# Shared experts as stationary weights over blocks of 512 tokens, and three residual norms worked out tile by tile

## What is computed

```python
x = layernorm(x + attention(x))      # 16 heads of 16, causal; keys and values from a latent of 64; rotary on 12 of 16
t = x                                # (2048, 256)
scores = softmax(t @ gate_w.T)       # 16 experts, the best 2 per token
y = sum over e of swiglu(t, w1[e], w3[e], w2[e]) * weight_e   # inner width 176
z = swiglu(t, sw1, sw3, sw2)         # the shared experts, inner width 352
out = layernorm(x + y + z)
# swiglu(t, a, b, o) = (silu(t @ a.T) * (t @ b.T)) @ o.T
```

## Time and profile before

| what | value |
|---|---|
| time, 3 runs | 842.92 us median (840.75 to 847.7) |
| profiled execution | 841.11 us, of which the span from first to last instruction is 839.4 us |
| mean granted TensorE clock | 0.927 of full speed |
| busy share of the span | PE 87%, PEld 59%, DVE 67%, ACT 48%, POOL 29% |
| DMA | 76.99 MB, mean 92 GB/s |

### The profile page before, as it was taken

How to read it: one execution, slowest core, us unless ns; L and a number is a source line. 1 busy time by engine, 2 the same in 40 slices (tenths; PEclk the granted TensorE clock), 3 DMA queues, 4 the chain that set the end, 5 groups by cost and what they waited for, 6 DMA issues and landing times. The chain is left out here.

```text
span 839.4 us, 14305 instructions
## 1 busy us (share of the span) xinstructions
PE 729.1 (87%) x4309; PEld 491.7 (59%) x4310; DVE 561.3 (67%) x1374; ACT 403.3 (48%) x891; POOL 243.8 (29%) x327
## 2 busy tenths in 40 slices
PE   4579899999999999999999999992879999999930
PEld 4467675764755665566465656441469966667610
DVE  6745777878788877776878788103574455666645
ACT  3124463655665756676656667781423322222203
POOL 6316182341261043107100000111027413333323
PEclk9659898999999999999999999995799999999975
DMA  4754326140052006002500000004997223323244
GB/s 130 177 150 117 87 49 180 38 120 22 2 140 88 1 2 145 8 1 55 148 2 1 1 2 1 2 1 161 319 288 269 94 67 93 101 89 100 88 158 173
DMA packets 43596, 76.99 MB, mean 92 GB/s; under 512 B 5984, under 2 KB 23136, under 8 KB 42672
## 3 DMA queue, kind: packets, MB, share of 16 engines
q1 hardware_dynamic: 35919, 57.72, 25.3%
q0 software_dynamic: 5184, 14.72, 5.1%
q10 hardware_dynamic: 2432, 3.80, 1.2%
HBM read 42.40 MB, written 33.45 MB: 90 GB/s over the span
## 5 line engine op out<-in xcount | busy, mean ns | idle before, releaser
L560 ACT ACTIVATE probs<-scores 128x512 f32<-128x512 f32 (+3 forms) x609 | 288.3, 545 | 183.3 <-PE scores L689 167.5
L782 DVE TENSOR_REDUCE mx<-turn_ps 128x1 f32<-128x512 f32 (+3 forms) x576 | 304.8, 591 | 74.2 <-PE turn_ps L652 74.1
L652 PE MATMUL turn_ps<-k_stack,q_stack 96*128 96x512 f32 (+3 forms) x832 | 250.6, 365 | 14.0 <-issue 4.2
L689 PE MATMUL scores<-q_stack,k_stack 98*128 98x512 f32 (+3 forms) x609 | 232.9, 396 | 10.7 <-ACT probs L560 6.0
L652 PEld LDWEIGHTS turn_ps<-k_stack,q_stack 96*128 96x128 f32 x832 | 152.2, 202 | 90.4 <-issue 34.7
L689 PEld LDWEIGHTS scores<-q_stack,k_stack 98*128 98x128 f32 x609 | 117.8, 195 | 43.4 <-ACT probs L560 24.1
L709 PE MATMUL pv_ps<-probs,v_ones 128*17 128x512 f32 (+3 forms) x1280 | 135.4, 539 | 1.2 <-POOL probs L467 0.8
L467 POOL TENSOR_SCALAR_AFFINE_SELECT probs<-probs 128x512 f32<-128x512 f32 x64 | 40.6, 635 | 325.1 <-ACT probs L560 324.9
L1154 POOL DMA_INDIRECT token_y<-ys,dest x47 | 45.5, 968 | 99.2 <-DVE ys L1519 56.8
L709 PEld LDWEIGHTS pv_ps<-probs,v_ones 128*17 128x17 f32 x1280 | 29.2, 97 | 67.1 <-issue 33.4
L1276 PE MATMUL gu_ps<-w_up_sb,xg_t 128*128 x188 | 67.2, 480 | 0.4 <-ACT xg_t L1213 0.3
(11 more groups left out here) (159 smaller groups left out, 767.5 us busy)
## 6 DMA issues: line engine op xcount, KB each, us to landing
kq_split<-kq_stage SPq DMA_DIRECT2D x96, 128.0 KB, 2.4
k_stack<-kq_split SPq DMA_DIRECT2D x8, 768.0 KB, 6.2
q_stack<-kq_split SPq DMA_DIRECT2D x32, 192.0 KB, 4.8
xg<-slot_x SPq DMA_DIRECT2D x47, 130.0 KB
slot_x<-blank SPq DMA_DIRECT2D x11, 520.0 KB, 7.8
w_up_sb<-w_up SPq DMA_DIRECT2D x4, 1408.0 KB
w_dn_sb<-w_dn SPq DMA_DIRECT2D x4, 704.0 KB
x_raw<-xT SPq DMA_DIRECT2D x4, 512.0 KB, 5.7
```

What stands on the lines that cost most here:

```text
L560: nc.scalar.activation(probs[:, s % PROB_BUFS, h, off:CH], score_bank(n)[:, off:CH], ACT.Exp)\
L652: ins = nc.tensor.matmul(dst[:, at:at + keys], q_stack[0:STACK, u % 4, h, tile * P:(tile + 1) * P], k_stack[0:STACK, pair, kb * CH + k0:kb ...
L689: nc.tensor.matmul(score_bank(n)[:, off:CH], k_stack[:, 2 * g + h // 2, b * P:(b + 1) * P], q_stack[:, u % 4, h, off:CH], start=True, stop ...
L782: last = nc.vector.tensor_reduce(mx[:, u % 2, h * TPC + tile, column:column + 1], bank_of(bank)[:, at:at + keys], AX.X, ALU.max)
```

## The change

It has two parts.

**Norms of chunks 0 to 2.** `norm_at` keeps s for these three. DVE's work is cut by tile and laid over steps s to s+6: addition of tile i in quarter 0 and its statistics in quarter 2 of step s+i, the aggregation and variance in step s+4, one tile's normalisation in each quarter of step s+6. Each addition and each `bn_stats` is now linked. POOL takes the power in step s+4 and stores in step s+8. Chunk 3's norm is moved behind all steps, with additions and statistics of the four tiles in turn, each linked.

**Shared stage.** The two shared experts are taken as one of inner width 352, in groups of 128, 128 and 96 (`GROUPS`). An item is a block of 512 tokens and a group, so there are 12. The weights are stationary and the tokens move: `up_shared` makes 6 matmuls of 512 columns for gate into `gu_ps` and 6 for up into `ht_ps`. The result is already transposed, so `turn_hidden` falls away for these items. ACT (silu, high part) and DVE (product, low part) work on 512 columns. `down_shared` makes 12 matmuls of 256 columns per item (4 tiles, 3 parts), over three groups into both banks of `y_ps`. DVE takes a block with two additions of 512 columns. `RANKS_AT` becomes 1, and the routing parts are placed around items 0, 1 and 2. The host lays the shared weights out as `s_up` and `s_dn`. Only the last item's down product is left for the slot stage.

```diff
-    norm_at = {first_step[(c + 1) * UNITS_PER_CHUNK] + 3: c for c in range(NCH)}
+    NORM_POW, NORM_ROWS, NORM_STORE = TPC, TPC + 2, TPC + 4
+    norm_at = {first_step[(c + 1) * UNITS_PER_CHUNK] + 3: c for c in range(NCH - 1)}
...
+            def store_rows(c):
+                pool.wait_ge(x1_ready, TPC * (c + 1))
                 pool.dma_start(x1_dram[c * CH:(c + 1) * CH, :].rearrange("(p i) n -> p i n", p=P), summed[:])\
...
-                if s in norm_at:
-                    inverse_deviation(norm_at[s])
+                if s - NORM_POW in norm_at:
+                    inverse_deviation(norm_at[s - NORM_POW])
+                if s - NORM_STORE in norm_at:
+                    store_rows(norm_at[s - NORM_STORE])
...
+            def add_rows(c, i):
...
+                link(nc.vector.tensor_tensor(summed[:, i, :], attn[:, i, :], x_tok[:, i, :], ALU.add))
+            def row_stats(i):
+                link(nc.vector.bn_stats(stats[:, i, :], summed[:, i, :]))
...
+            def norm_part(s, k):
                 for i in range(TPC):
+                    if s - i in norm_at and k in (0, 2):
+                        row_stats(i) if k else add_rows(norm_at[s - i], i)
+                if s - NORM_POW in norm_at and k in (0, 2):
+                    row_variance() if k else row_moments()
+                if s - NORM_ROWS in norm_at:
+                    norm_rows(norm_at[s - NORM_ROWS], k)
...
+                    norm_part(s, k)
                 for u in range(UNITS):
                     if last_bank_at[u] == s:
                         fold_maxima(u)
-                if s in norm_at:
-                    variance(norm_at[s])
-                if s - 1 in norm_at:
-                    layer_norm(norm_at[s - 1])
+            for i in range(TPC):
+                add_rows(NCH - 1, i)
+                row_stats(i)
+            row_moments()
+            row_variance()
+            for i in range(TPC):
+                norm_rows(NCH - 1, i)
...
+GROUPS = (128, 128, 96)
+RANKS_AT = 1
...
             for n in range(SHARED):
-                gate_of(n, n % 2, n)
-                if n:
-                    hidden_high(n - 1)
+                shared_item(n)
...
+                for half, bank, done in ((0, gu_ps, pe_gate), (1, ht_ps, pe_up)):
+                    for m, (k, (a, w)) in enumerate(product(range(KT), PARTS)):
+                        last = nc.tensor.matmul(bank[0:rows, n % 2], shared_up[:, w, k, half, at:at + rows],
+                                                x1_t[:, a, k, b * CH:(b + 1) * CH], start=(m == 0), stop=(m == 3 * KT - 1))
+                    last.then_inc(done, 1)
...
+                pe.wait_ge(hidden_low, n + 1)
+                if g == 0 and b:
+
+                    pe.wait_ge(shared_taken, 2 * b)
+                for i in range(TPC):
+                    for m, (a, w) in enumerate(PARTS):
+                        last = nc.tensor.matmul(y_ps[:, i // 2, i % 2 * E:(i % 2 + 1) * E],
+                                                hidden_split[0:rows, n % 2, a, i * P:(i + 1) * P], shared_dn[0:rows, w, g, :],
...
             for n in range(SHARED):
                 up_shared(n)
-                if n >= 1:
-                    turn_hidden(n - 1, (n - 1) % 2, n - 1)
-                if n >= 2:
-                    down_shared(n - 2)
                 if n == RANKS_AT:
                     ranks()
+                if n >= 1:
+                    down_shared(n - 1)
...
+            before_hide = {0: (scale_probs, first_choice)}
+            after_hide = {0: (second_choice,), 1: (slots_of,), 2: (experts_of,)}
...
             for n in range(SHARED):
-                if n in stages:
-                    stages[n]()
-                hide(n, n % 2, n)
-                if n >= 1:
-                    split_hidden(n - 1)
-                if n >= 3 and n % 2:
-                    take_shared((n - 3) // 2)
+                for stage in before_hide.get(n, ()):
+                    stage()
+                wide_hide(n)
+                for stage in after_hide.get(n, ()):
+                    stage()
+                split_hidden(n)
+                if n % NG == 0 and n:
+                    take_shared(n // NG - 1)
```

More of the change, by code:

```diff
@@ L834, in normalise, with row_moments @@
                   .then_inc(dve_read, 1)
[L836 to L847, removed]
+            def add_rows(c, i):
+                if i == 0:
+                    dve.wait_ge(dve_read, by_dve[("out", c * UNITS_PER_CHUNK + UNITS_PER_CHUNK - 1)])
+                    dve.wait_ge(tok_loaded, 16 * (c + 1))
+                    if c:
+                        dve.wait_ge(x1_stored, 16 * c)
+                        dve.wait_ge(x1_ready, TPC * c)
+                link(nc.vector.tensor_tensor(summed[:, i, :], attn[:, i, :], x_tok[:, i, :], ALU.add))
+            def row_stats(i):
+                link(nc.vector.bn_stats(stats[:, i, :], summed[:, i, :]))
+            def row_moments():
                 for i in range(TPC):
@@ L998, in build_experts @@
         consts2_ready = sem("consts2_ready")
+        pe_gate = sem("pe_gate")
+        pe_up = sem("pe_up")
+        pe_shared = sem("pe_shared")
+        wide_silu_done = sem("wide_silu_done")
+        wide_hidden_done = sem("wide_hidden_done")
+        hidden_low = sem("hidden_low")
+        shared_taken = sem("shared_taken")
         pe_x1t = sem("pe_x1t")
@@ L1280, in up_shared @@
             def up_shared(n):
-                i, half = divmod(n, 2)
+                b, g = divmod(n, NG)
+                rows, at = GROUPS[g], g * P
                 if n >= 2:
-                    pe.wait_ge(hidden_done, n - 1)
-                for m, (k, (a, b)) in enumerate(product(range(KT), PARTS)):
-                    last = nc.tensor.matmul(gu_ps[:, n % 2, 0:2 * INTER], x1_t[:, a, k, i * P:(i + 1) * P],
-                                            shared_up[:, b, half, k, :], start=(m == 0), stop=(m == 3 * KT - 1))
-                last.then_inc(pe_gu, 1)
+                    pe.wait_ge(wide_hidden_done, n - 1)
+                for half, bank, done in ((0, gu_ps, pe_gate), (1, ht_ps, pe_up)):
[3 more added lines that the diff above has]
+                    last.then_inc(done, 1)
             def turn_hidden(n, par, n0):
@@ L1308, in down_shared @@
             def down_shared(n):
-                i, half = divmod(n, 2)
-                pe.wait_ge(ht_copied, n + 1)
-                if half == 0 and i >= 2:
-                    pe.wait_ge(y_taken, i - 1)
-                for m, (k, (a, b)) in enumerate(product(range(2), PARTS)):
-                    last = nc.tensor.matmul(y_ps[:, i % 2, 0:E], hidden_split[:, n % 2, a, k, :], shared_dn[:, b, half, k, :],
-                                            start=(half == 0 and m == 0), stop=(half == 1 and m == 5))
-                last.then_inc(pe_y, 1)
+                b, g = divmod(n, NG)
+                rows = GROUPS[g]
+                pe.wait_ge(hidden_low, n + 1)
[5 more added lines that the diff above has]
+                                                hidden_split[0:rows, n % 2, a, i * P:(i + 1) * P], shared_dn[0:rows, w, g, :],
+                                                start=(g == 0 and m == 0 and i % 2 == 0), stop=(g == NG - 1 and m == 2),
+                                                skip_group_check=True)
+                last.then_inc(pe_shared, 1)
             pe.wait_ge(weights_low, 3)
```

152 lines of the change are left out of this document (89 added, 63 removed).

## The result

The changed kernel takes 837.49 us (median of 20 runs, 835.73 to 842.33), the kernel before 841.92 (20 runs beside it). The ratio is 0.9941, 95% interval 0.9924 to 0.9959: 4.4 us less, where 10 to 12 were forecast. The profiled execution took 836.4 us with a span of 834.7, against 841.1 and 839.4.

A forecast was written before the change was run, and what follows sets the result against it. PE was taken as the bound, with the scatter ending last before the slots. From 841.1 us: norms -6.9, chunk 3 +1.0, earlier slots -7.4, clock +3.1, transpositions -0.2, giving 830.7, stated as 831; range 823 to 839.5.

The forecast's parts named there:

- Norms, gain 6.9 us: Norms of chunks 0 to 2: spreading DVE's work gains 6.9 us, with 1.5 us left per chunk.
- Sum 11.4 us, the most that this part can give: Old norms of chunks 0 to 2: PE's stalls and slow clock cost 11.4 us, the upper bound of the gain.
- no PE idle time over 1 us beside the three norms: Sign that the norms' part is right: PE never idles over 1 us beside the norms of chunks 0 to 2.
- Chunk 3, +1.0 us: Last chunk's norm: eight linked operations take 3.7 us where addition and statistics took 2.7, so 1.0 us more.
- Item of 4.12 us: Shared stage on PE: 12 up matmuls and 12 down matmuls make an item of 4.12 us, 12 items 49.4.
- Slot numbers 2.5 us earlier: Routing chain: slot numbers ready at 619.0 instead of 621.5, with half clock at the ranks.
- POOL issues the same 32 DMAs: load at 661.6: Scatter: unchanged 42.6 us from slot numbers to first gathering load, so the load comes at 661.6 instead of 664.05.
- Clock at the first slot, +3.1 us: Start of slot stage: PE's 4 us pause brings the clock to half speed, losing 3.1 us, bounds 0 and 8.
- The norm's stalls stay: Rival, norms of chunks 0 to 2: the same loss spread thin, gain 0, time 837.6 us; 14 in 100.
- The slow return: Rival, slot stage: starts at half clock for 16 us, losing 8 instead of 3.1, time 835.6 us; 6 in 100.
- the costlier spread: Rival, norms of chunks 0 to 2: DVE's 5.6 us exposed three times, 5.4 us lost, time 843; 4 in 100.
- the half clock through the shared stage: Rival, shared stage: clock falls in PE's pauses and stays at half, slots 25.3 us later, time 860.5; 4 in 100.

The follow-up runs named there:

- shared_only: The changed kernel with the norms of chunks left as they were before the change; 836.85 us, ratio 0.9936 to the kernel before.
- psum_hidden: The changed kernel with the shared product written in place in PSUM, so DVE's low-part subtraction reads one PSUM operand; 834.91 us, ratio 0.9913 to the kernel before.
- after_again: The changed kernel, unaltered, measured a second time on another group's chip; 836.88 us, ratio 0.995 to the kernel before.
- dose_sbuf: psum_hidden plus two unused linked DVE operations per shared item, with both inputs in SBUF; 832.02 us, ratio 0.9881 to the kernel before.
- the twins: dose_sbuf and a kernel differing only in that its two added operations read one operand from PSUM; 832.02 and 832.49 us.

## Why the prediction was wrong in size

Most of the mechanisms came as forecast, the gain was less than half. Two terms failed: the price of the old norms, and the scatter at no change. Point by point:

- **Norms, gain 6.9 us: wrong.** The step that failed is "Sum 11.4 us, the most that this part can give". Measured is 7.7 in all. Chunk 0 was priced 5.2, of which 2.1 for a pause and 3.1 for a fall of the clock. Without any norm both come too: PE then stands 2.17 us for `q_stack`, and the clock is at half for 3.4 us. The stretch gives 1.5, which is no more than it varies by. For chunks 1 and 2 the price was 6.2, and 2.1 + 4.1 were measured. What was left is 0.8 + 1.5 + 2.3 = 4.6 where 3 x 1.5 was forecast: right in sum, and for chunk 0 by luck. The gain is then 3.1 us, or 1.5 against `shared_only`'s burst. The sign "no PE idle time over 1 us beside the three norms" failed at chunk 0, for the load.
- **Chunk 3, +1.0 us: right**, 3.66 against 2.67. By the sentence of the Trainium skill (VectorE: DVE Perf Modes, The DRAIN you can't avoid) that a semaphore costs nothing extra it would have been +0.6. Linked operations of 256 columns follow each other here at 0.46 us, four unlinked statistics take 1.41, 0.35 each, so the measurement decides. The page measured `tensor_copy`. No run has the links without the split.
- **Item of 4.12 us: right**, 4.18. PE's matmul of 512 columns costs 1.39 / 6 = 0.232 us; 0.226 was estimated.
- **Slot numbers 2.5 us earlier: right**, 2.6, the half clock at the ranks included (their 16 matmuls took 1.99 us; 1.12 in the earlier trace rows).
- **"POOL issues the same 32 DMAs: load at 661.6": wrong.** The DMAs are the same, but what DVE does beside them isn't: 45.2 us instead of 42.3. This is +3.0 us on the path, since the scatter ends last, as forecast. The same scatter at 42.3 us, in `psum_hidden`, gives them back. PE waited 7.86 us and not 4 for the same reason, for the most part: 4.92 in `psum_hidden`.
- **Clock at the first slot, +3.1 us: right in kind**, 2.4 in the changed kernel's profile and 1.1 in `after_again` (4.91 against 3.8).
- **Rivals.** "The norm's stalls stay" (part 1 gives 0, 837.6) came nearest in time. By the profiles of before and after the part gives 3.1, so the number is met by two halves: this rival in half, and a scatter that no rival held. The slow return, the costlier spread and the half clock through the shared stage did not come: the clock is 1.00 from 620 to 660.

The sum with the measured terms: -3.1 + 1.0 - 4.8 (-2.6 + 3.0 - 5.2) + 2.4 = -4.5, and the spans differ by 4.7. That this closes so well is in part luck, since the lines that the change does not touch differ by up to 1.1 us either way.

## What to carry to other kernels

The price of a stall is what its stretch takes without the cause, not the pause and the slow clock that one sees beside it. An experiment that leaves the work out is the surest; next best is to ask whether the neighbour that one compares with has the same work, and whether another wait lies right under the first. When a change leaves an engine's instructions alone but alters what runs beside them, their durations are not safe: list the new operations of DVE beside a POOL that issues DMAs, and look where their operands lie. A wait that has become the last one is worth a second look, for here one operand moved to PSUM gave 3.0 us, about as much as the whole new norm at best.

## What the runs showed of the hardware

- An indirect DMA issue on POOL takes 0.96 us. When it begins inside a DVE operation with two SBUF inputs it takes up to 1.57 us; the excess is the rest of that operation less some 0.12 us (0.51 us left: 1.35; 0.33 left: 1.17). Such an operation that starts 0.04 us or more behind the issue's start neither lengthens it nor is lengthened (0.69 us each in `dose_sbuf`, at 0.33 us into an issue). The Trainium skill (SBUF — State Buffer, Who interferes with whom) says that a DVE instruction with two SBUF inputs contends with a GpSimd instruction that reads SBUF, and one with at most one such input, outside DVE's 2-port modes, doesn't. The issue here takes its row numbers from `slot`, which lies in SBUF, and the twins agree. By this rule and the 0.69 us of the subtraction the scatter's line would have had a cost. The same section also says that a probe did not see `tensor_tensor` stall a DMA, and infers that descriptors need only the other interface; by that the cost would be nothing. In these runs a `tensor_tensor` does lengthen the issue, and the measurement decides.
- TensorE's clock fell to 1.2 GHz (0.53 from 662 to 672) behind a pause of 7.86 us at the first slot. It fell there in all eight profiles with a pause of 4.92 to 9.10 us, and not behind one of 0.85, 1.00 or 1.25 us. At chunk 0's norm it falls somewhere from 134 to 152 us in ten of the fourteen profiles, for 3 to 7 us; the changed kernel's own profile is one of the four without it (1.00 from 134 to 150), though PE stood 2.32 us there.
- A matmul on `q_stack` begins 0.09 us behind the landing of the load that it waits for, in twelve profiles. The load itself takes 5.6 to 7.3 us from issue to landing at that place.
